# The start of a RoPE attention: its sums moved from GpSimd to VectorE, one piece of look-ahead, and the weights' low parts in front of the statistics

## What is computed

```python
x = x + _L0_ffn_ref(_layernorm(x), ...)          # mixture of experts; its results are gathered by token
proj = layernorm(x) @ W_in.T + b_in               # (8, 512, 3 * 16 * 64)
q, k, v = split(proj)                             # 16 heads of 64
q, k = rope(q, sin, cos), rope(k, sin, cos)       # y_lo = lo*cos + hi*sin; y_hi = hi*cos - lo*sin
att = softmax(q @ k.T / 8, causal); y = att @ v
x = x + y @ W_out.T + b_out
```

## Time and profile before

| | |
|---|---|
| median of three runs | 2315.21 us (2312.51 to 2317.20) |
| the profiled execution's own time | 2315.66 us |
| its span | 2313.90 us |
| PE (TensorE matmul) busy | 1965.5 us, 85% |
| DVE (VectorE) busy | 1723.1 us, 74% |
| ACT (ScalarE) busy | 1398.9 us, 60% |
| POOL (GpSimd) busy | 1036.8 us, 45% |
| mean granted clock of TensorE | 0.936 of 2.4 GHz |
| chain that ended last: PE, issue | 10%, 1% |

### The profile page before, as it was taken

One profiled execution on the slowest core, in us unless ns is written; L12 is line 12 of the kernel. 1 busy time (PEld: TensorE's weight loads), 2 busy tenths in 40 slices (PEclk: granted clock), 3 DMA queues, 4 the chain that ended last, 5 costly groups with the idle time before them and its releaser, 6 DMA issues. The chain is left out here.

```text
span 2313.9 us, 52728 instructions
## 1 busy us (share of the span) xinstructions
PE 1965.5 (85%) x18758; PEld 1405.2 (61%) x18759; DVE 1723.1 (74%) x3717; ACT 1398.9 (60%) x2736; POOL 1036.8 (45%) x1231
## 2 busy tenths in 40 slices
PE   2889989899862999378799999999999999549999
PEld 1666666666561666145577777676767777426665
DVE  4778888788791444468678787879696977679997
ACT  1666666666562444267668696868787878344443
POOL 4435534355014000488747576657575663132222
PEclk9999999999955999689999999999999999869999
DMA  7000000000033332002100000000000000100000
GB/s 241 2 1 2 2 2 2 2 2 2 3 128 127 98 91 79 12 11 35 22 1 2 2 2 2 2 1 2 1 2 2 2 2 2 38 1 14 18 18 23
DMA packets 53114, 57.77 MB, mean 25 GB/s; under 512 B 7121, under 2 KB 47217, under 8 KB 52897
## 3 DMA queue, kind: packets, MB, share of 16 engines
q1 hardware_dynamic: 46240, 45.00, 6.2%
q0 software_dynamic: 6656, 9.85, 2.0%
HBM read 36.22 MB, written 18.61 MB: 24 GB/s over the span
## 5 line engine op out<-in xcount | busy, mean ns | idle before, releaser
L371 PE MATMUL a_bank<-w_in_sb,xnT_sb 128*128 128x512 f16 x1152 | 293.7, 394 | 33.7 <-DVE t_buf_sb L579 26.4
L1116 DVE TENSOR_REDUCE neg_max_sb<-a_bank 128x1 f32<-128x128 f32 (+3 forms) x512 | 236.1, 485 | 92.6 <-PE a_bank L896 88.7
L531 DVE TENSOR_REDUCE neg_max_sb<-a_bank 128x1 f32<-128x128 f32 (+3 forms) x512 | 236.1, 482 | 92.6 <-PE a_bank L288 91.1
L1039 ACT ACTIVATE probT_sb<-a_bank 128x512 f32<-128x512 f32 (+1 forms) x384 | 198.8, 526 | 145.3 <-PE a_bank L919 140.5
L442 ACT ACTIVATE p_hi_sb<-a_bank 128x384 f16<-128x384 f32 (+1 forms) x384 | 205.3, 535 | 120.7 <-PE a_bank L297 119.0
L434 ACT ACTIVATE prob_sb<-a_bank,neg_max_sb 128x128 f32<-128x128 f32 (+3 forms) x512 | 261.4, 543 | 23.9 <-DVE neg_max_sb L531 23.0
L538 DVE TENSOR_TENSOR p_lo_sb<-a_bank,p_hi_sb 128x384 f16<-128x384 f32 (+1 forms) x384 | 228.0, 595 | 59.7 <-ACT p_hi_sb L442 56.1
L453 ACT ACTIVATE stack_sb<-a_bank 128x1024 f16<-128x1024 f16 (+1 forms) x256 | 211.4, 826 | 7.0 <-PE a_bank L342 6.6
L297 PE MATMUL a_bank<-ident_f_sb,prob_sb 128*128 128x128 f32 x1280 | 206.4, 276 | 3.7 <-DVE p_lo_sb L538 3.1
L707 POOL TENSOR_TENSOR rope_w_sb<-t_buf_sb,sin_sb 128x256 f32<-128x256 f32 x128 | 146.0, 1140 | 134.7 <-DVE t_buf_sb L579 132.2
L371 PEld LDWEIGHTS a_bank<-w_in_sb,xnT_sb 128*128 128x128 f16 x1152 | 104.9, 100 | 143.0 <-DVE t_buf_sb L579 34.2
(11 more groups left out here) (268 smaller groups left out, 5613.3 us busy)
## 6 DMA issues: line engine op xcount, KB each, us to landing
sorted_rows<-zeros_sb SPq DMA_DIRECT2D x1, 4992.0 KB, 21.6
x_in_sb<-sorted_rows SPq DMA_DIRECT2D x39, 128.0 KB, 2.1
sorted_results<-y_moe_sb SPq DMA_DIRECT2D x39, 128.0 KB, 1.7
x_sb_sb<-L_attn_x SPq DMA_DIRECT2D x8, 512.0 KB, 10.7
w_raw_sb<-L_ffn_gate_bank SPq DMA_DIRECT2D x8, 512.0 KB, 3.6
w_raw_sb<-L_ffn_up_bank SPq DMA_DIRECT2D x8, 512.0 KB, 4.7
w_raw_sb<-L_ffn_down_bank SPq DMA_DIRECT2D x8, 512.0 KB, 5.8
out<-x_sb_sb SPq DMA_DIRECT2D x32, 128.0 KB, 1.7
```

The lines of the kernel that those rows point to most:

```text
L371: last = pe.matmul(out, xnT[:, x, c, j * P:(j + 1) * P], w["in"][:, w_, c, cols], start=k == 0, stop=k == len(terms) - 1)
L531: last = dve.tensor_reduce(neg_max[:, i:i + 1], S[(3 * h + g) % 2][:, off:off + L], AX.X, ALU.max, negate=True)
L1039: act.activation(probT[:, (h // 4) % 2, h % 4, T_AT[r]:T_AT[r + 1]], ST[(3 * h + r) % 2][:, 0:T_AT[r + 1] - T_AT[r]], ACT.Exp).then_inc(s_ ...
L1116: last = dve.tensor_reduce(neg_max[:, h % 2, i:i + 1], S[(3 * h + g) % 2][:, off:off + L], AX.X, ALU.max, negate=True)
```

## The change

VectorE's prologue makes the RoPE sum of piece p - 1 after it has taken piece p (`rope_sum`, eight sums in all), waiting for GpSimd's two products through a new semaphore, `s_w`. GpSimd's `rotate` in the prologue ends with the products, without its own step semaphore and without the sum, and its low part of piece p - 1 comes after the products of piece p. `rope_w` still has one buffer, so the products of piece p wait for the sum of piece p - 1. In the loop nothing is changed. In the block before the attention, VectorE's two low-part instructions of the weights now stand in front of its wait for the gathers, the statistics and the variances.

```diff
+    s_w = sem("rope_sin_ready")
@@ VectorE's prologue
             for p in range(PIECES):
                 take("piece", 0, 0, p)
+                if L1 and 1 <= p <= 8:
+                    rope_sum(p - 1)
+        def rope_sum(p):
+            wait(dve, s_w, p + 1)
+            wait(dve, s_u, p + 1)
+            wait(dve, s_piece, p - 1)
+            dve.tensor_tensor(rope_z[:, p % 2, :, :], rope_u[:, p % 2, :, :], rope_w[:, :, :], ALU.add).then_inc(s_z, 1)
@@ GpSimd
-        def rotate(b, half, p):
+        def rotate(b, half, p, prologue=False):
-            own(pool.tensor_tensor(rope_w[:, :, 32:64], src[:, :, 0:32],
-                                   sin[:, 32:64].unsqueeze(1).to_broadcast([P, 8, 32]), ALU.mult))
+            second = pool.tensor_tensor(rope_w[:, :, 32:64], src[:, :, 0:32],
+                                        sin[:, 32:64].unsqueeze(1).to_broadcast([P, 8, 32]), ALU.mult)
+            if prologue:
+                second.then_inc(s_w, 1)
+                return
+            own(second)
@@ GpSimd's prologue
-                    rotate(0, 0, p)
-                    piece_lo(0, 0, p)
+                    rotate(0, 0, p, True)
+                    if p:
+                        piece_lo(0, 0, p - 1)
+                    if p == PIECES - 1:
+                        piece_lo(0, 0, p)
@@ the block before the attention, VectorE
-            partial_stats(dve, 0)
-            variances(dve, GROUP_A)
             for c in range(C):
                 dve.wait_ge(s_hi, c + 1)
                 dve.scalar_tensor_tensor(out=w_in[:, 1, c, :], in0=w_raw[:, c, :], scalar=W1_SCALE,
                                          in1=w_in[:, 0, c, :], op0=ALU.mult, op1=ALU.subtract)
+            partial_stats(dve, 0)
+            variances(dve, GROUP_A)
             invert(dve, GROUP_A)
```

## The result

The changed kernel took 2300.02 us in the median (2294.59 to 2306.24, 6 runs), the kernel before 2314.47 (2312.51 to 2319.47, 6 runs). The ratio is 0.9937, 95% interval 0.9917 to 0.9958: faster by 14.6 us, with 9.7 to 19.2 in the interval. That is 0.6%, small but clear of no change. The profiled execution took 2305.93 us, its span is 2304.1 against 2313.9.

A forecast was written before the change was run, and what follows sets the result against it. The attention's start was taken as bound by a two-link chain, its body by TensorE; 8.1 us from the RoPE sums plus 2.9 from the weights' low parts, 11.0 together, gave 2304.5 us, range 2297 to 2309.5.

The forecast's parts named there:

- the two links: Start of L1 attention: weights and statistics, then eight RoPE pieces, a chain nothing runs beside; 2.9 and 8.1 us saved.
- First period: RoPE pieces: from GpSimd's first product of piece 0 to that of piece 1, 3.28 us.
- nobody is late through it at either clock: RoPE pieces: TensorE, one piece ahead with two banks, needs 2.74 + 0.15 us, less than a period, so delays nobody.
- The period, 3.79: RoPE pieces: GpSimd's time per piece with waiting for VectorE, 3.79 us, six times 22.74.
- The turns: RoPE pieces and gather issues: GpSimd and two-SBUF-input VectorE instructions alternate; a second product then ends 1.21 us after the first.
- The end, 5.63: RoPE pieces: from the products of piece 7 to the end of the last low part, 5.63 us.
- Part two, 2.9: Weights' low parts before the statistics: 6.1 us gained, 3.2 lost to later gather issues, 2.9 net.
- rival B: Gather DMAs: descriptors stop under the weights' low parts; total gain 7.4 us, 2308.3; chance 0.15 with another case (2306.5).
- Rival A: Both links: VectorE's sum and GpSimd's work run beside each other, DMAs not moved; gain 22.9 us, 2292.8; chance 0.05.
- its half: RoPE pieces: some turns missed, period near 3.1 us, time about 2299; chance 0.12.
- rival C: RoPE pieces: the loop is not shortened, period 4.86 us, only the low parts' move gains; 2312.8; chance 0.05.
- rival D: Attention body: TensorE's granted clock falls at another moment; each 0.01 costs 7 us, 2322 at 0.025 less; chance 0.03.

The follow-up runs named there:

- e0: The changed kernel executed again without edits; ratio 0.9933 to the kernel before, median 2296.71 us against 2311.61.
- e9: Changed kernel with the weights' low parts in one instruction of 6144 columns; profile only: 18.56 us from first high part to normalization, 31.21 from first product to last low part.
- e5: Changed kernel with the prologue's cosine product written to PSUM, so the sum has one SBUF input; profile only, first product to last RoPE low part 25.63 us.
- e6: As e5, with the cosine table also copied to PSUM, so no VectorE instruction of the pieces has two SBUF inputs; ratio 0.9910 to the kernel before.
- e1: Kernel before with only RoPE's sums on VectorE and GpSimd one piece ahead; weights' low parts stay behind the statistics; ratio 0.9950 to the kernel before.
- e2: Kernel before with only the weights' low parts moved in front of the statistics; ratio 0.9989 to the kernel before.
- e3: Kernel before with only GpSimd's low part one piece later, sums still on GpSimd; ratio 0.9977 to the kernel before.
- e8: e6 and e7 together in the changed kernel; ratio 0.9909 to the kernel before, median 2286.14 us against 2310.51.
- e7: Changed kernel with the weights' low parts in eight instructions of 768 columns instead of two of 3072; profile only, first high part to first normalization 13.80 us.

## Why the prediction held, step by step

- *The start isn't TensorE's, the two links are the path.* Right: the change in the two stretches, 12.1 us, is within the interval of the runs' difference, and "between" stayed at 10.5.
- *First period* 3.28: it was 3.49, as TensorE's second piece came 0.24 later to VectorE than in the trace of before (2.10 us behind the first instead of 1.86). So "nobody is late through it at either clock" is wrong for this one period: in it TensorE's clock made 3.21 to 3.75 of it in e0, the first profile and e9, which all have this order. For the other periods it is right.
- *The period, 3.79*: it was 3.66. The terms, in the prediction's order: products 0.72 + 1.21 = 1.93, measured 1.82; low part to its end 1.13, measured 1.15; sum behind it 0.64, measured 0.54; release 0.09, measured 0.15. The turns were sized from a wait in the loop; here each cost some 0.1 less. e5 and e6 showed the mechanism by taking one and then both turns away: 3.66, 2.93, 2.48.
- *The end, 5.63*: 5.49. The sum of stretch two is 3.49 + 6 x 3.66 + 5.49 = 30.95 (rounded) against 31.65, the gain 8.8 against 8.1.
- *Part two, 2.9*: 3.3. The order of the issues came out as walked: the second before VectorE, the third and fourth each behind one low part, 3.03 and 2.96. The predicted landing was 13.4 us after the stretch's start, the measured one 13.1.
- *The skill's rule and rival B.* The Trainium skill, in "SBUF — State Buffer", section "SBUF: two separate sides", lets the descriptors of GpSimd's DMAs wait for as long as VectorE runs a two-port perf-mode instruction. For this two-input instruction e9 shows otherwise in the middle of an issue: the third issue ran its last 0.64 us under it and took its usual 1.54. The same section says that the loser of the shared ports blocks until the other's instruction has ended, and lists instructions with two SBUF inputs among those that take them, against a GpSimd instruction that reads SBUF. e5 and e6 agree with it for the sum, 1.62 against 0.69, and e9 for the fourth issue, 7.04 against 1.54. An issue did not hold VectorE in the same way: the low parts of e9 began under the third issue and took 6.56 us for 6144 columns, not more than the 6.63 of the two halves.
- *Rival A* (no turns) and its half are out by the rows after, with a period of 3.66 and issues of 3.03 and 2.96; *rival C* (the period stays) by the same; *rival D*, the clock, did not make the kernel slower, but it is the size that I had too small. I wrote that a body that differs by more than 2 us would be something that none of my steps has. It differed by 4.8, and the same kernel again differed by 3.7 from its own first profile. That bound came from three runs within 4.7 us; the 23 runs of before in the later comparison span 13.5.
- *The time.* 2304.5 against a median of 2300.0, inside the range. Of the 4.5 us, 1.1 are the sizes above, 0.7 are that the kernel before came out lower with three more runs (2314.47 against 2315.21), and 0.3 are the step from 2304.2 to 2304.5. The other 2.4 are not shown by any part: e0 gave 15.5 us by its ratio again, with an interval from 11.6 to 19.4, whose low end is below the stretches' 12.1. Over the other kernels the gain by ratio lies on both sides of the one by stretches: 11.6 against 9.1 in e1, 2.5 against 3.3 in e2, 5.3 against 5.1 in e3, 20.8 against 20.7 in e6, 21.0 against 23.0 in e8. Whether the change gains anything outside the two stretches stays open; the profiles show none. How near the median comes is in part chance: beside e0 the same two kernels had medians of 2311.61 and 2296.71.

## What to carry to other kernels

When work is moved from GpSimd to VectorE to run beside GpSimd, count each VectorE instruction with two SBUF inputs as GpSimd's time too, about 0.45 to 0.55 us for one of 0.69 here, or put one of its inputs into a free PSUM bank. A long instruction of this kind in front of GpSimd's DMA issues delays each by what is left of the instruction: cut it into pieces. And judge an edit of a few microseconds by its stretch between two landmarks of the trace, which repeated to 0.3 us (0.6 with e9's, all of it in the first period), where whole executions of one kernel spread over 10.

## What the runs showed of the hardware that I had not expected

- One operand in PSUM ended the waiting entirely: the sum of the same 512 f32 columns went from 1.62 us to 0.69 beside a GpSimd instruction, and the pair cosine product and sum, both with PSUM operands, left GpSimd's period at 2.48 us, its bare work (e6).
- In turns, the waiting engine got in at the end of the running instruction even when the other's next was already queued. In e7, with eight low parts back to back, no issue took over 2.30 us.
- TensorE's granted clock in stretch two rose from 0.75 to 0.93, with six matmuls every 3.7 instead of every 4.9 us. Behind the first period it brought nothing, since TensorE waits there at either level: in e0 and e1 the part of stretch two behind it is 27.47 us long in both, at 0.93 and 1.00. In the first period the moment at which 2.4 GHz came was worth up to 0.5 us.
